# Identity products between the units of the count-matrix stage of a fused graph network and mixture of experts

## What is computed

```python
def _edge_conv(x, src, dst, W, b):
    xi = x[dst]
    xj = x[src]
    m = jnp.concatenate([xi, xj - xi], axis=-1) @ W + b
    s = jax.ops.segment_sum(m, dst, num_segments=N)
    cnt = jax.ops.segment_sum(jnp.ones((dst.shape[0],), m.dtype), dst, num_segments=N)
    return s / jnp.maximum(cnt, 1.0)[:, None]
...
    for W, b in ((W0, b0), (W1, b1), (W2, b2)):
        h = jax.nn.relu(_edge_conv(h, src, dst, W, b))
        xs.append(h)
    cat = jnp.concatenate(xs, axis=-1)
    return cat @ Wf + bf
...
    x = x + _L0_gnn_ref(_layernorm(x, axis=-1), edge_index, L0_gnn_W0, ...)
    x = x + _L0_ffn_ref(_layernorm(x, axis=-1)[None], L0_ffn_Wg, ...)[0]
```

## Time and profile before

| | |
|---|---|
| median of 3 runs | 215.17 us (214.72 to 218.1) |
| the profiled execution | 214.7 us |
| its span, first to last instruction | 212.9 us |
| TensorE busy | 172.5 us, 81% of the span |
| VectorE busy | 112.6 us, 53% |
| ScalarE busy | 69.1 us, 32% |
| mean granted clock of TensorE | 0.959 |

### The profile page before, as it was taken

One profiled execution on the slowest core, in us unless ns is written; L12 is line 12 of the kernel. 1 busy time (PEld: TensorE's weight loads), 2 busy tenths in 40 slices (PEclk: granted clock), 3 DMA queues, 4 the chain that ended last, 5 costly groups with the idle time before them and its releaser, 6 DMA issues.

```text
span 212.9 us, 3627 instructions
## 1 busy us (share of the span) xinstructions
PE 172.5 (81%) x1129; PEld 145.2 (68%) x1130; DVE 112.6 (53%) x288; ACT 69.1 (32%) x185; POOL 47.7 (22%) x73
## 2 busy tenths in 40 slices
PE   0351367759989999999999799999999999999810
PEld 0230266648979798989999699887777777786600
DVE  5499698786057455235354789635252433425200
ACT  4282595644021144116210450133223232414200
POOL 7014000001950093030000200003232323323232
PEclk9999999956999999999999999999999999999985
DMA  5600050000012003999950588000323222222222
GB/s 133 182 12 0 2 136 16 2 0 3 2 51 103 8 0 54 296 368 366 366 186 0 163 263 304 11 5 0 33 23 42 23 26 25 25 25 25 25 25 25
DMA packets 14646, 17.84 MB, mean 84 GB/s; under 512 B 1586, under 2 KB 11428, under 8 KB 14500
## 3 DMA queue, kind: packets, MB, share of 16 engines
q1 hardware_dynamic: 12580, 15.75, 23.2%
q0 software_dynamic: 1872, 1.70, 7.0%
q10 hardware_dynamic: 176, 0.14, 0.5%
HBM read 15.12 MB, written 2.48 MB: 83 GB/s over the span
## 4 chain that ended last, share of the span: by engine, by line
PE 68%; DVE 17%; DMA 6%; issue 4%; ACT 1%; POOL 1%; ACTq 1%; POOLq 0%; DVEq 0%
PE bank L1490 10%; PE cnt_ps L1504 8%; PE bank L1358 5%; PE bank L1484 4%; PE bank L1482 4%; DVE hot_lo L817 4%; DMA out_rows<-y_sb,row_now 3%; PE cnt_ps L1358 3%; PE bank L1211 3%; PE cnt_ps L1218 3%; PE bank L1213 3%; PE bank L1212 3%; PE cnt_ps L1497 2%; PE g_ps L1211 2%; DMA dst_chunk<-in_dst 2%
## 5 line engine op out<-in xcount | busy, mean ns | idle before, releaser
L576 POOL DMA_INDIRECT out_rows<-y_sb,row_now x13 | 20.3, 1562 | 31.9 <-DMA out_rows<-y_sb,row_now 18.9
L1504 PEld LDWEIGHTS cnt_ps<-w_sb,h_t 128*128 128x128 f32 x104 | 19.7, 190 | 8.9 <-issue 6.8
L1504 PE MATMUL cnt_ps<-w_sb,h_t 128*128 x104 | 24.7, 380 | 0.9 <-ACT h_t L745 0.9
L1490 PE MATMUL bank<-w_sb,xt 128*128 x52 | 24.5, 594 | 0.0
L1151 DVE TENSOR_TENSOR h_pre<-bank,b_bc 128x512 f32<-128x512 f32 x12 | 8.3, 692 | 29.7 <-PE bank L1490 29.7
L1259 PE MATMUL bank<-hot_key,hot_lo 125*128 125x45 bf16 (+4 forms) x80 | 8.5, 244 | 18.3 <-DVE hot_key L820 9.2
L1259 PEld LDWEIGHTS bank<-hot_key,hot_lo 125*128 125x128 bf16 x80 | 5.4, 124 | 21.2 <-DVE hot_key L820 13.5
L1482 PE MATMUL bank<-hot_slot,x_hi 128*128 128x256 f32 x70 | 18.3, 301 | 0.0
L1484 PE MATMUL bank<-hot_slot,x_lo 128*128 128x256 f32 x70 | 16.9, 281 | 0.0
L817 DVE TENSOR_TENSOR hot_lo<-iota_lo,edge_rel 125x1024 bf16<-125x1024 int16 x20 | 13.7, 683 | 2.1 <-PE g_ps L1259 2.0
L745 ACT COPY h_t<-cnt_ps 128x512 f32<-128x512 f32 x13 | 7.6, 585 | 21.9 <-PE cnt_ps L1497 21.9
(11 more groups left out here) (263 smaller groups left out, 422.7 us busy)
## 6 DMA issues: line engine op xcount, KB each, us to landing
w_sb<-in_L_ffn_W SPq DMA_DIRECT2D x16, 512.0 KB, 9.8
b_bc<-in_L_ffn_b SPq DMA_DIRECT2D x8, 256.0 KB, 4.8
w_stage<-in_L_gnn_W SPq DMA_DIRECT2D x3, 512.0 KB, 3.9
w_stage<-in_L_gnn_Wf SPq DMA_DIRECT2D x4, 256.0 KB, 4.3
b_bc<-in_L_ffn_b SPq DMA_DIRECT2D x1, 1024.0 KB, 11.0
x_sb<-in_x SPq DMA_DIRECT2D x1, 512.0 KB
out_rows<-x_sb SPq DMA_DIRECT2D x1, 512.0 KB
out_rows<-y_sb,row_now POOLq DMA_INDIRECT x13, 3.8
```

What stands on the lines that cost most here:

```text
L576: pool.indirect_dma_start(out=out, out_offset=bass.IndirectOffsetOnAxis(ap=row_now[:, h:h + 1], axis=0), in_=y_sb[:, h, :], in_offset=None ...
L1490: last = pe.matmul(bank[1][:, :], xt[:, k, h * P:(h + 1) * P], w1_sb[:, ds(e, 1), k, :], start=k == 0, stop=k == KC - 1)
L1504: last = pe.matmul(bank[3][:, 0:D], h_t[:, k, :], w2_sb[:, ds(e, 1), k, :], start=k == 0, stop=k == HC - 1)
```

## The change

Behind each of the 16 units of turns 3 and 4 TensorE gets three identity products, into `g_ps[0]`. That bank is last read at the transposes ahead of turn 2 and next written at line 1300. The other turns call `sum_unit` as before. No other engine's instructions change.

```diff
+WARM_SUM = 3
...
-            def sum_turn(g):
+            def sum_turn(g, between=0):
                 for u in range(g * UNROLL, (g + 1) * UNROLL):
                     sum_unit(u)
+                    for _ in range(between):
+                        pe.matmul(g_ps[0][:, 0:P], ident[:], ident[:], start=True, stop=True)
...
-            sum_turn(3)
+            sum_turn(3, WARM_SUM)
             ys_product(0, 2)
-            sum_turn(4)
+            sum_turn(4, WARM_SUM)
```

## The result

The changed kernel takes 226.06 us (median of 4 runs, 225.78 to 226.17), the kernel before, beside it, 215.57 us (4 runs, 214.72 to 218.1). The ratio is 1.045, with an interval of 1.040 to 1.051. That is slower, as forecast, but by 10.5 us instead of 4.4, and outside the range of 217.7 to 222.7.

What follows compares the result with a forecast made beforehand. TensorE was taken to bound the kernel: 10.7 us of identity products, minus 5.15 of room, minus 1.5 from the clock, plus 0.35 of waiting, +4.4. Forecast median 219.6 us; range 217.7 to 222.7, 8 in 10.

Steps and rivals of the forecast that it cites:

- the forecast's own band: Whole kernel: slower by +3.4 to +5.8 us, given a chance of 0.68.
- Price of an identity product: Turns 3 and 4 on TensorE: two records 0.112 us apart, 0.223 us a product, 0.67 for three, 10.7 for 48.
- The third rival: Turns 3 and 4: identity products cost 0.11 us each, a unit some 0.68; total 215.7 us; 0 to +3.4, chance 0.11.
- The unit: Four count products plus three identity products on TensorE: 1.00 us in turn 3, 1.04 in turn 4.
- The clock's rise: Early in turn 3: TensorE's clock goes to full speed at 38.3 us, so only unit 24 starts at the lower clock.
- the first rival: Turn 3: clock rises 2 to 3 us late, or units cost more; +5.8 to +8 us, chance 0.15.
- The second rival: Turns 3 and 4: the lower clock stays through both; about +18 us, 233 us, chance 0.04.
- Start of turn 3: TensorE's first count product of turn 3 starts at 37.85 us, as before.
- VectorE's chain and the wait for pair 18: Behind turn 3: 5.25 us until VectorE has pair 18 ready, at 51.2; TensorE waits 0.35 us for it.
- The shift goes through whole: From the bias products to the end: every later line comes +4.4 us later, with nothing lost or gained.

Runs made afterwards that it cites:

- after_whole_block: Changed kernel plus 32 one-column bf16 products in idle time ahead of turn 1, 256 instructions more than the kernel before; 221.24 us, ratio 1.021.
- after_8_more: Changed kernel plus four one-column products ahead of turn 1, 200 instructions more than the kernel before; 223.94 us, ratio 1.033.
- one_wide_product: Changed kernel with one fp32 product of 384 columns behind each unit in place of three of 128, 64 instructions added; 220.03 us, ratio 1.016.
- code_only: Kernel before plus 96 one-column bf16 products (192 instructions) in idle time ahead of turn 1, no identity products in turns 3 and 4; 220.02 us, ratio 1.016.
- after_late_weights: Changed kernel with SyncE's loads of the experts' weights held until level 2's last features are ready, TensorE's code unchanged; 219.83 us, ratio 1.015.
- code_late_weights: Kernel before plus 96 one-column products (192 instructions), with the experts' weight loads held until level 2's last features; 218.00 us, ratio 1.011.

## Why the prediction was wrong

The sign and the mechanism of the two turns were right, and their +5.3 lies in the forecast's own band (+3.4 to +5.8). The step that failed is a later one: "all that follows on TensorE is the same dense work ... Nothing ends at a fixed time there, so the shift goes through to the end whole."

**Price of an identity product: right.** A record is 0.11 to 0.12 us apart at full clock and 0.21 at the lower one; the six of a unit and what lies between take 0.70 of the chain, for 0.67 + 0.08 - 0.05 in the working. The third rival, cheap products, is out: with them a unit would be 0.68 us, and it is 1.02. The rule of the Trainium skill behind it (TensorE: Matmul & The Clock Gate, section "Back-to-back issue gap") gives about 56 ns for an isolated gap, and about 81 ns for a sustained stream of weight loads and matmuls; a record of an fp32 product takes 0.112 us here, so neither holds for it.

**The unit: 1.00 and 1.04 forecast, 1.025 and 1.05 measured.** With the shorter last unit of a turn it comes to 7.10 us for the seven units that follow the first in turn 3, for 7.00, and to 4.13 for the last four of turn 4, for 4.15.

**The clock's rise: 38.3 forecast, near 39.3 measured.** The first unit took 1.51 us instead of 1.10: +0.41. It is the late clock of the first rival, in its mildest form, and a matter of the execution: in after_whole_block, after_8_more and one_wide_product the clock is full from 37.6 to 37.9 on, no unit takes 1.5 us, and the bias products start at 56.8 to 57.1. The trace's record of the clock puts the short rise of before at 38.3, inside the prediction's bounds. The second rival, that it doesn't hold, is out: from there to the end of turn 4 the two levels of the identity records show no other fall.

**Start of turn 3: same forecast, 0.23 later.** Nothing changed ahead of it; it is a difference between two executions. Together with the terms above: 0.23 + 0.41 + 0.10 for the rest of turn 3 is 0.74, and it ends at 46.69 instead of 45.95.

**VectorE's chain and the wait for pair 18: right.** 5.25 us forecast, 5.29 measured; the wait of TensorE is there. Units 36 to 39 take 4.13 us for 4.15. The bias products start at 57.71 instead of 56.85, the shift is 5.3 instead of 4.4, and 0.74 of the missing 0.86 is turn 3; the rest is hand-overs. With this alone the forecast would have been 220.5, inside the range; one_wide_product, which has the work without the late block, is at 220.03.

**"The shift goes through whole": wrong.** Two terms, against the kernel before:

- the wait for code, and the low clock behind it. Idle time in level 2 is 2.87 us instead of 0.29, +2.6. Behind it the clock is at its lower level for 6.8 us; what TensorE does in that time would take about half at the full clock, +3.4 at most. An idle time of 0.66 us at 60.96, between the degrees and level 0, is gone, as the branch there takes 0.34 us for 2.78: -0.8 (a shift of 4.47 instead of 5.28 at the sums of level 0). The sum is +5.2 at most; measured is +4.8 (65.02 less 60.19). In code_only, with 3.4 us at the lower clock, the same terms give 60.19 + 2.6 + 1.7 - 0.8 = 63.7, and 63.73 is measured.
- a second fall of the clock, at 134.9. It costs 1.2 us (14.81 less 13.65). after_late_weights does not have it, but after_whole_block, whose hole is 1.0 us, has one at its like place, 130.1, and code_only and after_8_more, with holes of 2.9 and 3.3 us, have none. Its cause stays open; TensorE is busy there in all, and the 20 products of 8 columns ahead of it (132.45 to 134.6 in the kernel after) stand in the kernels without the fall too.

That the hole is a late block of code, and late because of the experts' loads, is shown by three results that need each other: the code moved without the work makes it (code_only), the work without the moved code doesn't (one_wide_product), and holding the loads back takes it away with the code unchanged (after_late_weights, code_late_weights). That the hole makes the clock fall is the order in the windows in each kernel that has a hole over 2 us, and it was not tried apart from it.

The profile of before had a sign of it that I passed over: it has an idle time of 0.66 us at 60.96 and one of 0.29 at 93.28, both with nothing waited for, and an instruction queue in its third part (q8, 11 packets). The three level branches of TensorE in its trace take 2.8 to 3.4 us (0.33 us in the kernel after, where the target is at hand), and products in the queue cover all of it but these idle times. The Trainium skill describes the mechanism: in Runtime: NRT & Kernel Launch, section "Instruction fetch mechanics", instructions come in 16 KiB blocks of 256 through a DMA queue of their own, a taken branch out of the window at hand forces a fetch, and a crossing is mostly hidden. This case's trace agrees on the blocks (16 KB a packet), and on the fetch; that it is mostly hidden holds for before (0.66 and 0.29 us open) and not for the kernels with 192 or 200 instructions more, where 2.9 to 3.3 us lay open. A forecast that had asked "what does a later block cost, if it isn't hidden", with the branch of 3.4 us as the price, would have had a rival at 219.6 + 3.4 = 223.0 us, and above it if the clock falls in the gap.

Still open: where on its way the packet loses the 2.1 to 2.9 us under the loads (its own transfer takes 1.15 us with them and 0.94 without); why it comes 1.7 us behind the branch in after_whole_block and 0.9 in before; and what makes runs of the kernel before differ by some 1%.

## What to carry to other kernels

Added instructions move all code behind them against its blocks, and that can cost more than they do: count them, look in the trace of before for branches that take microseconds and idle times that wait for nothing, and ask what hides each and which loads fill the DMA at that moment. Before a small edit is judged by its time, give it a twin that has its instructions and not its work (one-column products in an idle place), and one with its work and other instructions. And products put into idle time are free only as long as the block of them ends before the engine that is on the path needs it: one product a unit cost nothing here, three (or one as wide) cost 1.5 to 2% where the code did not come late, and none of the versions beat the kernel before.

## What the runs showed of the hardware

- **A branch of TensorE whose block isn't there yet** took 2.8 to 3.4 us in before and up to 4.1 in after_whole_block; from branch to code it was 6.4 to 6.5 us under the weight loads in all kernels with 192 or 200 instructions more, as branch or as branch and what follows it. With the block at hand a branch took 0.34. The packet of 16 KB started 4.0 us after the branch with the DMA at 360 to 380 GB/s and 1.1 with it idle; TensorE had the code 2.3 to 2.7 us after the packet's start.
- **Eight instructions** (200 instead of 192) move the wait from a gap behind 0.3 us of branch into the branch itself; the idle time of TensorE only goes from 2.87 to 3.29 us.
- **A gap of some 3 us costs more than itself:** the clock fell near its end (0.4 us ahead of it in the kernel after, 0.9 and 1.1 behind it in code_only and after_8_more) and stayed low for 6.8, 3.4 and 3.4 us, though the work behind the gap was dense.
- **A product of 384 columns costs what three of 128 do:** a unit with it takes 1.00 us, with three products 1.02; but it is two pairs of instructions instead of six.
